# First norm inside the first projection, adjacency turned two tiles later, and an earlier half of each sum in the relation

## The reference, cut to what matters

```python
h = jnp.maximum(_layernorm(x, axis=-1), 0.0)
x = x + _L0_gnn_ref(h, adj, ...)     # seq = h @ W_seq; scores from seq @ a1, seq @ a2 per head;
                                     # softmax over the neighbours in adj, times seq, @ W_out, elu
...
h = jnp.maximum(_layernorm(x, axis=-1), 0.0)
x = x + _L3_gnn_ref(h, adj, ...)     # 8 heads: scores q k^T at listed pairs, softmax over neighbours,
                                     # mean over the heads, times h
```

## Time and profile before

| | |
|---|---|
| median of 3 runs | 4329.72 us (4329.33 to 4334.23) |
| profiled execution | 4338.02 us, its span 4336.3 us |
| busy in the span | PE 3594.6, DVE 3571.6, ACT 2553.4, POOL 1425.2 us |
| mean granted clock of TensorE | 0.91 |
| first norm, first projection, relation | 38.1, 113.2, 849.3 us |

### The profile page before, as it was taken

One profiled execution on the slowest core, in us unless ns is written; L12 is line 12 of the kernel. 1 busy time (PEld: TensorE's weight loads), 2 busy tenths in 40 slices (PEclk: granted clock), 3 DMA queues, 4 the chain that ended last, 5 costly groups with the idle time before them and its releaser, 6 DMA issues. The chain is left out here.

```text
span 4336.3 us, 55622 instructions
## 1 busy us (share of the span) xinstructions
PE 3594.6 (83%) x20081; PEld 2079.6 (48%) x20136; DVE 3571.6 (82%) x5848; ACT 2553.4 (59%) x3008; POOL 1425.2 (33%) x1417
## 2 busy tenths in 40 slices
PE   6888889879788848687887889899988968888887
PEld 3688888634344424243343344677764423333333
DVE  4799999769999996699999925899984079998996
ACT  3566666459888885588897723454443344444442
POOL 0444100007887795399988811000002000000000
PEclk9999999989998969899898899999999978888888
DMA  4611100221110100511101043000002121111110
GB/s 149 246 29 27 29 29 22 67 55 46 46 45 28 34 20 22 168 39 42 29 20 42 17 135 137 24 18 16 19 21 89 40 83 39 49 44 44 44 44 15
DMA packets 160245, 228.82 MB, mean 53 GB/s; under 512 B 85137, under 2 KB 96288, under 8 KB 154672
## 3 DMA queue, kind: packets, MB, share of 16 engines
q1 hardware_dynamic: 148592, 191.33, 13.7%
q0 software_dynamic: 11376, 33.76, 2.1%
HBM read 158.48 MB, written 66.47 MB: 52 GB/s over the span
## 5 line engine op out<-in xcount | busy, mean ns | idle before, releaser
L1695 DVE SCALAR_TENSOR_TENSOR junk<-expd,mid 128x2048 bf16<-128x2048 f32 x440 | 1036.5, 2356 | 13.8
L579 ACT ACTIVATE steepz<-s1b,thr_h 128x1024 bf16<-128x1024 f32 (+1 forms) x768 | 669.9, 927 | 484.3 <-DVE mask L646 471.4
L732 PE MATMUL acc<-V,mask 128*128 128x198 bf16 (+1 forms) x5504 | 747.1, 274 | 121.8 <-DVE mask L646 70.0
L1595 ACT ACTIVATE junk_s<-expd,nmid 128x2048 bf16<-128x2048 f32 x264 | 528.9, 2003 | 130.0 <-POOL nmid L1655 116.4
L732 PEld LDWEIGHTS acc<-V,mask 128*128 128x128 bf16 x5504 | 478.7, 99 | 190.3 <-DVE mask L646 78.9
L1598 ACT ACTIVATE junk_s<-expd,nmid 128x2048 bf16<-128x2048 f32 x264 | 528.0, 2000 | 0.0
L2140 PE MATMUL psS<-KT,qs 64*128 64x512 f32 x1024 | 382.3, 740 | 156.7 <-DVE m L2250 152.3
L739 PE MATMUL acc<-V,adjT 128*128 128x99 bf16 (+1 forms) x5504 | 453.0, 220 | 0.0
L646 DVE TENSOR_TENSOR mask<-steepz,adjT 128x1024 bf16<-128x1024 bf16 (+1 forms) x768 | 398.1, 552 | 11.3 <-PE acc L732 4.5
L739 PEld LDWEIGHTS acc<-V,adjT 128*128 128x128 bf16 x5504 | 368.8, 99 | 49.8 <-issue 1.4
L1467 PE MATMUL psX<-parts,block 128*128 128x512 bf16 x1481 | 354.6, 393 | 13.5 <-DMA block<-adj_dram 10.7
(11 more groups left out here) (306 smaller groups left out, 5800.5 us busy)
## 6 DMA issues: line engine op xcount, KB each, us to landing
rows<-in_adj_dram SPq DMA_DIRECT2D x32, 1024.0 KB, 5.1
s1b<-sT_dram SPq DMA_DIRECT2D x32, 512.0 KB, 3.8
block<-adj_dram SPq DMA_DIRECT2D x32, 512.0 KB, 4.4
adj_dram<-adjT POOLq DMA_DIRECT2D x4, 2048.0 KB, 20.6
rel_table<-zeros POOLq DMA_DIRECT2D x64, 128.0 KB, 19.3
y_dram<-yo SPq DMA_DIRECT2D x32, 256.0 KB, 2.0
step_dram<-xo SPq DMA_DIRECT2D x32, 256.0 KB, 2.0
A<-step_dram SPq DMA_DIRECT2D x8, 1024.0 KB, 13.5
```

Source lines behind the costliest of these rows:

```text
L579: act.activation(steepz[:, m % RELUS, :], s1b[:, q % 4, :], ACT.Relu, bias=thr_h[:, u, 1, j:j + 1], scale=STEEP).then_inc(relu_ready, 1)
L732: mm = pe.matmul(acc[:, c % 2, i // TB, o:o + 2 * W], mask[:, j % RING, tile(i)], V[:, u, j, 0:2, :].rearrange("p s w -> p (s w)"), start= ...
L1595: act.activation(junk_s[:, 0, :], expd[:, slot[i], :], ACT.Relu, bias=col(nmid, i), accum_out=col(above, i)).then_inc(sums_ready, 1)
L1695: link(dve.scalar_tensor_tensor(junk[:, :], e, col(mid, i), e, ALU.is_gt, ALU.mult, accum_out=col(mass, i)))
```

## The change

`norm_stage` is removed and its work goes into the projection, now `norm_project_stage`, with `RowNorm`. SP loads three chunks of x, then W and the vectors, then waits until four tiles are normed and loads the last chunk into the first chunk's place (`xs` has twelve tiles), then the adjacency rows. VectorE takes the statistics of all tiles first, in groups of four, and folds `w12` later, two of eight parts ahead of each of the first four `turned`. ScalarE does four ReLUs, then in each of the first eight steps two copies of turned tiles and two ReLUs of later tiles, with a root for a group where it is due. TensorE turns two tiles of h at the start of each of the first eight steps. A row tile of the adjacency is cast and turned in step t + 2 and not t; the last two stand behind the last step. `ROWS_FIRST`, `ROWS_AFTER` and SP's order of the row loads and of `sT`, `top` and `m2` stay as they are. `psS` takes the place of one of the norm's PSUM buffers, `sT` that of `xs`.

In the relation `apply` does half a group, two products; the first half stands ahead of `scores(t, m, 1)`, the second behind it.

```diff
-    def norm_stage(self, x_dram, nat, tr):
...
-    def project_stage(self, H, DH, w_dram, a1_dram, a2_dram, seq, tr, g, adj_dram=None):
+    def norm_project_stage(self, H, DH, x_dram, w_dram, a1_dram, a2_dram, seq, tr, g, adj_dram):
...
+            xs = self.sb(st, "xs", [P, 3 * NT // 4, D])
-            sT = self.sb(st, "sT", [2 * H, N])
+            sT = xs[0:2 * H, 0:4, :].rearrange("p t d -> p (t d)")
...
-            psS = self.ps(st, "psS", [P, NT, 2 * H])
+            norm = RowNorm(self, st, seq, tr)
+            psS = norm.ps[:, 0, :, :].rearrange("p k i -> p (k i)")[:, 0:NT * 2 * H].rearrange("p (t h) -> p t h", t=NT)
+            x_in = [self.sem(st, f"x_in{c}") for c in range(4)]
+            names_done = self.sem(st, "ident_done")
...
+                def load_x(c):
+                    b = 4 * (c % 3)
+                    sp.dma_start(xs[:, b:b + 4, :], x_dram[4 * c * P:4 * (c + 1) * P, :].rearrange("(t p) d -> p t d", p=P)
+                                 ).then_inc(x_in[c], 16)
+
+                for c in range(3):
+                    load_x(c)
...
+                sp.wait_ge(norm.h_ready, 4)
+                load_x(3)
...
+                for t in range(NT):
+                    if t % 4 == 0:
+                        dve.wait_ge(x_in[t // 4], 16)
+                    norm.moments(dve, link, t, xs[:, t % 12, :])
+                    if t % 4 == 1 and t >= 5:
+                        norm.scale(dve, link, t // 4 - 1)
+                norm.scale(dve, link, NT // 4 - 1)
+                dve.memset(shift[:, :], SHIFT)
                 dve.wait_ge(w_in, 16 * KD)
                 dve.wait_ge(a_in, 32)
-                for k in range(KD):
-                    for i in range(2):
-                        link(dve.tensor_tensor(prod[:, :].rearrange("p (h d) -> p h d", h=H),
-                                               w[:, k, :].rearrange("p (h d) -> p h d", h=H),
-                                               avec[:, i, :, :].to_broadcast([P, H, DH]), ALU.mult))
-                        link(dve.tensor_reduce(w12[:, k, i, :], prod[:, :].rearrange("p (h d) -> p h d", h=H),
-                                               AX.X, ALU.add))
-                dve.memset(shift[:, :], SHIFT).then_inc(w12_ready, 1)
+
+                def fold(n):
+                    k, i = n // 2, n % 2
+                    link(dve.tensor_tensor(prod[:, :].rearrange("p (h d) -> p h d", h=H),
+                                           w[:, k, :].rearrange("p (h d) -> p h d", h=H),
+                                           avec[:, i, :, :].to_broadcast([P, H, DH]), ALU.mult))
+                    dve.tensor_reduce(w12[:, k, i, :], prod[:, :].rearrange("p (h d) -> p h d", h=H),
+                                      AX.X, ALU.add).then_inc(w12_ready, 1)
+                    dve.wait_ge(w12_ready, n + 1)
...
-                if adj_dram is not None:
-                    for t in range(ROWS_FIRST - 2):
-                        turned(t)
+                for t in range(ROWS_FIRST - 2):
+                    if t < KD:
+                        fold(2 * t)
+                        fold(2 * t + 1)
+                    turned(t)
...
+                def cast_rows(t):
+                    act.wait_ge(adj_in[t % 2], 16 * (t // 2 + 1))
+                    if t >= 2:
+                        act.wait_ge(a_ready, 2 * (t - 1))
+                    act.activation(rows16[:, t % 2, :], rows[:, t % 2, :], ACT.Copy,
+                                   accum_out=deg[:, t:t + 1]).then_inc(cast, 1)
+
+                norm.root(act, 0)
+                for t in range(4):
+                    norm.relu(act, t, xs[:, t % 12, :])
+                for t in range(NT + 2):
+                    if 2 * t < NT:
+                        norm.copy(act, 2 * t)
+                        norm.copy(act, 2 * t + 1)
+                        if t + 1 < NT // 4:
+                            norm.root(act, t + 1)
+                        if 2 * t + 4 < NT:
+                            norm.relu(act, 2 * t + 4, xs[:, (2 * t + 4) % 12, :])
+                            norm.relu(act, 2 * t + 5, xs[:, (2 * t + 5) % 12, :])
+                    if t >= 2:
+                        cast_rows(t - 2)
+                    if t < NT:
+                        act.wait_ge(seq_ready, t + 1)
+                        act.copy(seq[:, t, :], psQ[:, t % 2, :]).then_inc(seq_copied, 1)
...
-                pe.wait_ge(w_in, 16 * KD)
+                pe.wait_ge(names_done, 2)
 
                 def sequence(t):
+                    if 2 * t < NT:
+                        norm.turn(pe, 2 * t)
+                        norm.turn(pe, 2 * t + 1)
+                    if t == 0:
+                        pe.wait_ge(w_in, 16 * KD)
+                    pe.wait_ge(norm.n_copied, t + 1)
                     if t >= 2:
                         pe.wait_ge(seq_copied, t - 1)
                     for k in range(KD):
                         mm = pe.matmul(psQ[:, t % 2, :], tr[:, k, tile(t)], w[:, k, :],
                                        start=(k == 0), stop=(k == KD - 1))
                     mm.then_inc(seq_ready, 1)
-                    if adj_dram is not None:
-                        turn_rows(t)
+                    if t >= 2:
+                        turn_rows(t - 2)
...
-                pe.wait_ge(w12_ready, 1)
+                pe.wait_ge(w12_ready, 2 * KD)
+                pe.wait_ge(norm.n_copied, NT)
...
+                turn_rows(NT - 2)
+                turn_rows(NT - 1)
...
-                def apply(t, gp):
-                    if gp == 0 and t >= 1:
+                def apply(t, gp, half):
+                    if gp == 0 and half == 0 and t >= 1:
                         pe.wait_ge(xo_ready, t)
                     pe.wait_ge(t_copied, 4 * t + gp + 1)
-                    for j in range(4 * gp, 4 * gp + 4):
+                    for j in range(4 * gp + 2 * half, 4 * gp + 2 * half + 2):
                         mm = pe.matmul(psO[:, :], attnT[:, j, :], nat[:, j, :], start=(j == 0), stop=(j == NT - 1))
-                    if gp == 3:
+                    if gp == 3 and half == 1:
                         mm.then_inc(o_ready, 1)
 
                 for t in range(NT + 2):
@@ -2168,12 +2135,15 @@
                             scores(t, m, 0)
                         if t >= 2:
                             transposes(t - 2, m)
+                        if t >= 2 and m >= 1:
+                            apply(t - 2, m - 1, 0)
                         if t < NT:
                             scores(t, m, 1)
                         if t >= 2 and m >= 1:
-                            apply(t - 2, m - 1)
+                            apply(t - 2, m - 1, 1)
                     if t >= 2:
-                        apply(t - 2, 3)
+                        apply(t - 2, 3, 0)
+                        apply(t - 2, 3, 1)
```

More of the change, by code:

```diff
@@ L318, in project_stage, with _ @@
             dve_done = self.sem(st, "dve_done")
[L319 to L336 removed]
+            rows = self.sb(st, "rows", [P, 2, N])
+            rows16 = self.sb(st, "rows16", [P, 2, N], BF16)
+            ident16 = self.sb(st, "ident16", [P, P], BF16)
+            deg = self.sb(st, "deg", [P, NT])
+            psA = self.ps(st, "psA", [P, 2, NT // 2, P], BF16)
+            adj_in = [self.sem(st, f"adj_in{c}") for c in range(2)]
+            cast = self.sem(st, "cast")
+            a_ready = self.sem(st, "a_ready")
+            a_copied = self.sem(st, "a_copied")
+            id_done = self.sem(st, "id_done")
+            block = st.enter_context(nc.Block())
+            @block.gpsimd
+            def _(pool):
+                self.identity(pool, chain(pool, names_done), self.ident)
+                link = chain(pool, id_done)
+                self.identity(pool, link, ident16)
             @block.sync
             def _(sp):
+                def load_x(c):
[4 more added lines that the diff above has]
+                    load_x(c)
                 if len(w_dram.shape) == 3:
@@ L354, in load_rows @@
                     sp.dma_start(rows[:, t % 2, :], adj_dram[tile(t), :]).then_inc(adj_in[t % 2], 16)
-                if adj_dram is not None:
-                    for t in range(ROWS_FIRST):
-                        load_rows(t)
+                for t in range(ROWS_FIRST):
+                    load_rows(t)
                 sp.wait_ge(sT_copied, 4)
-                sp.dma_start(g.sT_dram[0:2 * H, :], sT[:, :]).then_inc(sT_out, 16)
+                sp.dma_start(g.sT_dram[0:2 * H, :], sT).then_inc(sT_out, 16)
                 sp.wait_ge(top_ready, 1)
@@ L364, in _ @@
                 sp.dma_start(m2[:, :], g.top_dram[H:2 * H].partition_broadcast(P)).then_inc(m2_in, 16)
-                if adj_dram is not None:
-                    for t in range(ROWS_FIRST, NT):
-                        load_rows(t)
+                for t in range(ROWS_FIRST, NT):
+                    load_rows(t)
                 sp.wait_ge(sT_out, 16)
@@ L398, in _ @@
                 dve.wait_ge(s_copied, 1)
```

(22 more changed lines are left out.)

90 lines of the change are left out of this document (3 added, 87 removed).

## The result

The changed kernel takes **4290.5 us** (median of 4 runs, 4284.1 to 4293.3) against 4330.5 us before (4 runs, 4329.3 to 4334.2): ratio **0.9905**, 95% interval 0.9891 to 0.9918, so 40 us or 0.9% less. The profiled execution took 4293.3 us with a span of 4291.5, against 4338.0 and 4336.3.

The account below looks back on a forecast made before the run. No engine was taken to be busy throughout, each stage having its own limit. Gains of 21 us in the projection and 22 in the relation summed to 43, giving a median of 4287 us (profiled 4295), range 4266 to 4306.

Parts of the forecast that it names:

- Steps 2 to 5: Early projection: a chain through ScalarE and TensorE, 6.15 us a step against TensorE's own 4.38 + 1.0.
- What was costed at nothing: Projection: `fold` (11 us if uncovered), SP's wait before x's last chunk, aliased `psS` and `sT`, POOL's second identity: no cost.
- The step that gives back: Projection's end: rows cast two steps later delay the maximum and rows 13; last copy at 124.8, stage gain 21 us.
- The bound of 32: Projection's upper bound: with the row chain hidden, the end would be 113.9, a gain of 32 us.
- the fourth pair's wait: Relation: second scores now stand behind two products too, a wait of 0 to 0.5 us, taken as 0.4.
- full clock: Relation case: third pair's scores ready at 3951.0, before VectorE asks at 3952.8; no wait, 3.3 us gained.
- low until the scores: Relation case, clock low until 3953.0: new wait of 2.2 us, third pair's scores 0.2 more, 0.8 us gained.
- 4271: Rival, relation: the clock comes back early, wait falls to 0.4, 6 us in all, gain 38 + 21; chance 0.14.
- 4304: Rival, relation: gives nearly nothing, wait moving whole before the second pair's scores; gain 5 + 21; chance 0.13.
- 4297: Rival, projection: gives only about 11 us, ScalarE's longer queue and the row chain taking the rest; chance 0.10.
- 4474: Rival, relation, slower: low clock does not end, 11.8 us a tile, 165 in all; decides from some 17 us; chance 0.05.
- One sign of being wrong: Listed as showing the prediction wrong: w landing after 18, a longer early beat, or a low clock beyond 12 us a tile.

Follow-up runs that it names:

- rows_first: Against the changed kernel, SP issues all sixteen adjacency row tiles before `sT`, the maximum and m2, not thirteen: 4288.5 us, ratio 0.9894 to the kernel before.
- first_pair_split: Against the changed kernel, only the first group's products are split around the second pair's scores, later groups stand whole behind: 4293.1 us, 0.9916 to the kernel before.
- finish_early: Against the changed kernel, VectorE finishes the earlier tile (y and `xo`) one place sooner in the relation: 4279.3 us, ratio 0.9885 to the kernel before.

## Why the prediction was right

Forecast were 4287 us, range 4266 to 4306, with 21 us from the projection and 22 from the relation; measured 4290.5, and in the profiles 21.6 and 22.2. The profiled execution was put at 4295 and took 4293.3.

- **Start.** The first product was put at 15.5 and came at 15.38, though it took 6.28 us where later ones take 3.60; steps 0 and 1 ended at 25.80 against 25.0. Steps 2 to 5: 6.15 forecast, 5.98 measured. `psR` at 60.35 against 60.6, its end at 74.20 against 74.5. The overlap allowed for ScalarE's operations was right to 0.2 us a step: the chain through both engines was the right model, though its slack is only 0.59 us. The measured 21.6 us for the whole projection are known to some 3 us (20.7 between the means of the marks).
- **What was costed at nothing.** `fold`, the aliased buffers and SP's wait ahead of the last chunk show nowhere as a wait on the path up to `psR`.
- **The step that gives back.** Eleventh turn ended at 97.58 (97.7 forecast), cast of rows 13 at 114.71 (114.5), last copy at 124.27 (124.8). rows_first shows that this step was the right one to name: with the rows issued first, 5.4 of the 10.9 us between the forecast end (124.8) and that of its upper bound (113.9) come back at the last copy. The bound of 32 was not reached because the rows' own landing and casting remain, 2.13 us of wait in front of rows 15.
- **The relation.** The new wait appeared where it was put, in the second pair's second half, behind TensorE's wait for `xo` and two products. It was put at 1.2 us a tile and is 1.60 (22.4 / 14, without the first tile's wait), and the fourth pair's wait, put at 0.4, does not exist. The two errors cancel by luck: 22.4 forecast, 22.4 measured in these tiles. The mean of the cases "full clock" and "low until the scores" was a fair choice, since the trace has both kinds of tile (0.99 and 2.06 us in those shown), but the better kind of tile was read too well: it was put at no wait, and there the clock falls as the wait for `xo` ends.
- **What was not said.** That the split of the first group alone does the work. The prediction's sum takes its whole gain from that split and gives the later ones only the cost of 0.4, but it treats the three as one edit. first_pair_split gives 19.9 us by itself, and the 2.3 that the other two add are within the scatter.
- **The middle.** Forecast unchanged, measured -1.0, well inside the 14 us over which that stretch varies. The whole kernel's 40 us are 3 less than forecast, also within that.

The rivals: the clock did not come back early (4271); the wait did move in front of the second pair, but by half and not whole (4304); the projection gave its sum and not 11 (4297); and the low clock always ended before the third pair (against 4474).

One sign of being wrong did appear, a low clock beyond 12 us in a tile. In the first tile shown it is low from 3601.2 to 3618.3, as long as the 17 us from which the slower case was to decide, and seven of the fourteen tiles have a wait like this tile's. It cost only those 2 us, because the stretch begins with the first pair, where VectorE does not wait for scores, and ends before the third: the third pair's scores take 1.99 us, full clock, in all fourteen tiles. The prediction counted its low stretch from 3942.8, within the second pair; that it may begin with the tile was not in it.

In that tile TensorE was busy for 14.80 of 16.8 us, with gaps of 1.20 and 0.52 us, and the granted clock had a mean of 0.52. The Trainium skill, "TensorE: Matmul & The Clock Gate", section "What you observe", has the full rate back shortly after sustained matmul activity begins; the trace agrees only if gaps like these break it. In the tile at 3657 the clock fell as an idle time of 2.77 us ended. The Trainium skill, "TensorE: Matmul & The Clock Gate", section "Why this matters for your kernels", warns of idle gaps between bursts of matmuls; the trace agrees, but how long a gap it takes no run here shows.

What is shown and what is only read: that the order of the products sets the waits is shown by kernels of equal work that fall into three groups wider apart than the scatter: 841.9 to 844.1 us with the first group whole behind the scores, 819.8 to 824.2 with two of its products ahead, 801.9 to 804.4 with one or none. That the half clock is what makes two products too long is read from the tiles' rows; no kernel here held the clock up with all else equal, so how the remaining 14.6 us of finish_early divide between clock and queue stays open.

## What to carry to other kernels

Work that can fill a wait should stand in the queue where the engine would wait anyway, and no longer than that wait: two products there gave 22 us, one gave 40, and of the three places only one was seen to matter. Moving a producer earlier is worth what the slowest thing queued behind it allows: 29 us of an earlier first product became 22 because loads stood behind a chain that had not moved as far (rows_first got 5.4 of them back at the last copy), so look at who issues what behind whom. A lag between two steps of a pipeline is also a decision on what stands behind the next stall.

## What the runs showed of the hardware

- In the tile at 3657 the granted clock fell to 0.50 after a stretch in which TensorE was busy for 2.57 of 6.40 us, with no single gap above 2.77 us, and two products then took 3.68 us, where four took 3.70 at full clock.
- A transfer of 32 values from SBUF was answered in 3.4 us when issued into a quiet queue (100.66 to 104.10), in 7.9 us behind a row tile of 1 MB and 256 KB of `sT` on SP's queue (108.55 to 116.47), and in 6.8 us on GpSimd's queue while the rows were loading (100.45 to 107.29).
- At the start the profile's granted clock and the durations disagree: the row of the first 25.8 us gives 1.00, but the first `psQ` takes 6.28 us and the next ones 3.60. The passes of the first begin some 0.85 us apart until 20.6 and those of the next 0.43 apart, a ratio of two, so in this stretch the clock's row is less to be trusted than the durations.
- Stages with the same code, from the first attention mask to the relation, took 3324.7 to 3338.8 us in thirteen profiles, a scatter of 0.4% between kernels that do not differ there.
